# Bias handling in a routed feed-forward: b1 by broadcast DMA and VectorE, b2 by GpSimd, no bias products on TensorE

## The chip, the cores and the metric

The kernel runs on one core of one Trainium2 chip. The metric is the device time in microseconds of one execution. Of several executions the median is given.

## The reference

One transformer block on 2 x 1024 tokens of width 256: cross-attention over 154 context rows (16 heads), then a feed-forward layer with 8 experts, of which each token takes the one with the highest router logit.

```python
x = x + xcond(layernorm(x), ctx, ctx, tau, delta, Wq, bq, Wk, bk, Wv, bv, Wo, bo)
# feed-forward of layernorm(x), DIM = 256, HIDDEN = 1024, E = 8
top1 = jnp.argmax(softmax(x @ router_w + router_b), axis=-1)
for i in range(E):
    h = jnp.einsum('bsd,df->bsf', x, w1[i]) + b1[i]
    a, g = jnp.split(h, 2, axis=-1)
    y = jnp.einsum('bsh,hd->bsd', a * jax.nn.sigmoid(g), w2[i]) + b2[i]
    out = out + jnp.where((top1 == i)[..., None], y, 0.0)
x = x + out
```

## The kernel before

The attention stage takes the first 170 us or so, and a routing stage follows that sorts the tokens by expert. The change hardly touches either. It lies in the feed-forward stage, which begins near 189 us.

Tokens are gathered into 18 tiles of 128 rows (`SLOT_TILES`). Thirteen are **whole**: all rows belong to one expert. Five are **mixed**, at places 2, 5, 8, 11 and 14 (`MIXED_AT`): four pieces of 32 rows, each with an expert of its own. The hidden width of 1024 is cut into four **quarters**; a quarter holds 256 hidden values with their 256 gates. The loop runs n = 0 to 71: all 18 tiles for quarter 0, then for quarter 1 and so on. The weights of one quarter for all experts (8 x 768 KB) are in SBUF, and those of the next are loaded meanwhile by SP (`load_experts`, L662). In quarter 0 SP paces the eight loads for quarter 1 by TensorE's transposes of the gathered tiles (`xin_ready`).

For a whole tile TensorE makes the up product with the hidden values on partitions (L1342). Its bias b1 is then one number for each partition: ScalarE adds it in the sigmoid (L1599), VectorE in the gating (L2022), and the down product (L1380) follows two steps later. ScalarE copies each whole tile's w1 to `w1_now` first (L1565).

For a mixed tile the tokens are on partitions, 32 for each piece, and the weights are the moving operand: the up product is 16 matmuls over four column strips of 32 (L1334), the down product 16 more (L1373). Before each, the pieces' w1 and w2 must be copied out of the quarter's weights to `piece_w1` and `piece_w2`: two pieces by VectorE (L2039, L2042), the others by ScalarE and GpSimd (L881, L884 on GpSimd; in quarter 0 it takes two pieces of the second to fifth mixed tile). VectorE multiplies value by gate to `mixed_u` (L2014), TensorE turns this (L1350), ScalarE copies it to `mixed_ut` (L1607), and the down product runs three steps after the up product. A bias here is a row for each piece, along the free dimension, and there are two ways in which it comes in:

- In quarter 0 both biases come from TensorE. b1 and b2 were split into three bf16 parts by GpSimd (`split_biases`), stored and loaded back to `b_split` by SP. `of_tile`, made by VectorE (L1975), says which of its 24 rows belong to a piece's expert. Four matmuls of 24 rows add the bias ahead of the up product (L1330, 512 columns) and four ahead of the down product (L1369, 256 columns). ScalarE's gate (L1592) and VectorE's `mixed_u` then read the PSUM bank.
- In quarters 1 to 3 SP loads the b1 row of each piece's expert, broadcast to 32 partitions, to `bias_in` (L734). VectorE adds it to the product and writes `hidden` in SBUF (`bias`, L2006). ScalarE's gate (L1587) and `mixed_u` read `hidden`.

The result y adds up in `slot_rows`: VectorE adds each quarter's down product (`add_y`, L2033). For whole tiles b2 comes in during quarter 1: GpSimd adds the expert's row to y (`add_b2`, L907) at step j + 19 for tile j, and VectorE's `add_y` of quarter 1 waits for this.

Each engine runs its own list of instructions in order. GpSimd's list in one step n of the loop is: a gather (L897, until all 18 are done), the copies of w2 and of w1 that are due, `add_b2`, and in the last quarter an output store (L912). An engine's number of an expert is read from SBUF to a register (L877 on GpSimd, L733 on SP) once and then kept.

Of the kernel before, what the change touches and what calls it, by code (L numbers as in the profile page):

```python
# [33 lines left out]
P = 128  # L34
# [48 lines left out]
PARTS = 3  # L83
BIAS_ROWS = PARTS * EXPERTS
TURN_B1, SPLIT_BIASES = (0, 21), (1, 6)
# [31 lines left out]
def constants():  # L117
# [20 lines left out]
        "row_expert": (p % EXPERTS)[:, None] * 1.0,  # L138
# [15 lines left out]
def build(nc, x, ctx_t, tau, delta, wq, bq, wk, bk, wv, bv, wo, bo, rw, rb, weights, b1, b2, const, ones, minus_ones, out,  # L154
# [3 lines left out]
    with ctx:  # L158
# [13 lines left out]
        of_tile = sb("of_tile", [BIAS_ROWS, WHOLE_TILES + MIXED_PIECES], BF16)  # L172
# [81 lines left out]
        biases = sb("biases", [P, P + DIM // HDIM], stack=splitting)  # L254
        biases_rest = sb("biases_rest", [P, P + DIM // HDIM], stack=splitting)
        bias_parts = sb("bias_parts", [P, PARTS, P + DIM // HDIM], BF16, splitting)
# [31 lines left out]
        b_split = sb("b_split", [BIAS_ROWS, 2 * HQ + DIM], BF16)  # L288
# [16 lines left out]
        b1_parts = nc.dram_tensor("b1_parts", (PARTS, P, P), BF16).ap()  # L305
        b2_parts = nc.dram_tensor("b2_parts", (PARTS, P, DIM // HDIM), BF16).ap()
# [17 lines left out]
        s_b2 = sem("s_b2")  # L324
        bias_step = sem("bias_step")
        bias_stored = sem("bias_stored")
        bias_loaded = sem("bias_loaded")
# [161 lines left out]

        def w2_due(n):  # L490

            return [mixed_count(n) - 1] if n >= 0 and mixed(n) else []
# [89 lines left out]
        def _(sp):  # L582

            def store_biases():
                sp.wait_ge(bias_step, 4)
                sp.dma_start(b1_parts.rearrange("w p n -> p w n"), bias_parts[:, :, 0:P]).then_inc(bias_stored, 16)
                sp.dma_start(b1_rows.rearrange("e (m n) -> (e m) n", n=P), biases[:, 0:P]).then_inc(bias_stored, 16)
                sp.dma_start(b2_parts.rearrange("w p n -> p w n"), bias_parts[:, :, P:]).then_inc(bias_stored, 16)

            def load_biases():  # L590
                sp.wait_ge(pv_done, UNITS * CHUNKS)
                sp.wait_ge(bias_stored, 48)
                for w in range(PARTS):
                    at = slice(EXPERTS * w, EXPERTS * (w + 1))
                    sp.dma_start(b_split[at, 0:2 * HQ],
                                 b1_parts[w].rearrange("(q e m) n -> e q (m n)", q=QUARTERS, e=EXPERTS)[:, 0, :]).then_inc(bias_loaded, 16)
                    sp.dma_start(b_split[at, 2 * HQ:],
                                 b2_parts[w].rearrange("(e a) n -> e (a n)", e=EXPERTS)).then_inc(bias_loaded, 16)
# [92 lines left out]
            sp.dma_start(biases[:, P:], b2.rearrange("(p n) -> p n", p=P)).then_inc(s_b2, 16)  # L691
# [44 lines left out]

            sp.dma_start(b2_sb[:, :, :].rearrange("p e n -> p (e n)"),
# [9 lines left out]
        def _(pool):  # L747
# [76 lines left out]
            def split_biases():  # L824
                pool.wait_ge(s_b2, 16)
                pool.wait_ge(b1_copied, 1)
                pool.tensor_copy(bias_parts[:, 0, :], biases[:, :]).then_inc(bias_step, 1)
                pool.wait_ge(bias_step, 1)
                pool.tensor_tensor(biases_rest[:, :], biases[:, :], bias_parts[:, 0, :], ALU.subtract).then_inc(bias_step, 1)
                pool.wait_ge(bias_step, 2)  # L830
                pool.tensor_copy(bias_parts[:, 1, :], biases_rest[:, :]).then_inc(bias_step, 1)
                pool.wait_ge(bias_step, 3)
                pool.tensor_tensor(bias_parts[:, 2, :], biases_rest[:, :], bias_parts[:, 1, :], ALU.subtract).then_inc(bias_step, 1)

# [6 lines left out]
            for c, i in SCHEDULE:  # L841
# [8 lines left out]
                if (c, i) == SPLIT_BIASES:  # L850
                    split_biases()
# [14 lines left out]
            for t in POOL_HOTS:  # L866
                pool.wait_ge(row_known, t // TPC - CHUNKS + 3)
                if t == POOL_HOTS[0]:
                    pool.wait_ge(bias_stored, 48)
# [9 lines left out]

            def copy_w1(k, c):  # L880
                pool.tensor_copy(piece_w1[:, c, :], w1_of_piece(pool, k, expert_of(piece_at(k, c)))).then_inc(w1_pool, 1)  # L881

            def copy_w2(k, c):
                pool.tensor_copy(piece_w2[:, c, :], w2_of_piece(pool, k, expert_of(piece_at(k, c)))).then_inc(w2_pool, 1)  # L884
# [15 lines left out]
            def add_b2(j):  # L900
                at = tile_at(j)
                expert = expert_of(at)
# [3 lines left out]
                y = slot_rows[:, at, DIM:2 * DIM]  # L906
                pool.tensor_tensor(y, y, b2_sb[:, bass.ds(expert, 1), :].rearrange("p o n -> p (o n)"), ALU.add).then_inc(b2_added, 1)  # L907
# [37 lines left out]
        def _(pe):  # L945
# [362 lines left out]
            def expert_rows(at, columns):  # L1308

                return of_tile[:, at:at + 1].to_broadcast([BIAS_ROWS, columns])  # L1310
# [805 lines left out]
```

## Time and profile before

| | |
|---|---|
| median of 3 runs | 412.96 us (412.38 to 413.06) |
| profiled execution, its own time | 413.04 us |
| its span | 411.2 us |
| TensorE busy | 380.7 us (93% of the span) |
| VectorE, ScalarE, GpSimd busy | 258.4, 220.4, 140.2 us |

The engines are called PE (TensorE), PEld (its weight loads), DVE (VectorE), ACT (ScalarE), POOL (GpSimd) and SP. The span is cut into 40 slices of about 10.3 us; a digit is the busy share in tenths, and PEclk the granted TensorE clock in tenths.

```profile
PE   7969999899999888978999999999999999999991
PEclk9979989999999999986999999999999999999996
```

TensorE is full in all slices from the twentieth to the last but one. Its clock falls once, at the turn from routing to feed-forward (slices 18 and 19).

### The profile page before, as it was taken

What the parts mean: (1) busy time and instruction counts of PE and PEld (TensorE: products, weight loads), DVE (VectorE), ACT (ScalarE), POOL (GpSimd) and SP (SyncE); (2) the same over time, 40 slices, a digit from 0 to 9 for tenths busy, and PEclk for the clock granted to TensorE, in tenths of its full rate; (3) what the DMA queues carried; (4) which work ended last, traced back from release to release, by engine and by line L of the source; (5) the groups of instructions that cost most, each with busy time, mean ns of one, the idle gap of its engine ahead of it and who ended that gap; (6) DMA issues with size and microseconds to landing.
All of it is one profiled execution on the core that took longest, in us unless ns stands there. A gap on an engine that the chain in (4) does not pass through costs nothing.

```text
span 411.2 us, 8873 instructions
## 1 busy us (share of the span) xinstructions
PE 380.7 (93%) x2907; PEld 263.1 (64%) x2912; DVE 258.4 (63%) x714; ACT 220.4 (54%) x433; POOL 140.2 (34%) x184
## 2 busy tenths in 40 slices
PE   7969999899999888978999999999999999999991
PEld 3545444456555444766776777887877778877680
DVE  3948985667777863886466634776556553665540
ACT  3314467656655566454555555666556565565540
POOL 5258150031011011367766431433511121155632
PEclk9979989999999999986999999999999999999996
DMA  7563769081101292134856562891039600001111
GB/s 222 127 185 75 146 141 274 6 181 52 50 26 53 84 376 72 63 109 139 313 189 219 152 225 62 301 383 48 27 97 421 175 27 28 0 34 60 38 65 38
DMA packets 29122, 54.33 MB, mean 132 GB/s; under 512 B 8482, under 2 KB 18774, under 8 KB 28950
## 3 DMA queue, kind: packets, MB, share of 16 engines
q1 hardware_dynamic: 25090, 45.72, 35.7%
q0 software_dynamic: 2688, 7.26, 5.5%
q10 hardware_dynamic: 1300, 0.79, 0.9%
q8 instruction: 24, 0.39, 0.4%
q14 instruction: 20, 0.16, 0.1%
HBM read 39.33 MB, written 6.99 MB: 113 GB/s over the span
## 4 chain that ended last, share of the span: by engine, by line
PE 77%; DVE 7%; ACT 4%; issue 4%; SPq 3%; DMA 2%; POOL 1%; another core or an unknown queue 1%; ACTq 0%; DVEq 0%; POOLq 0%
PE bank L1342 22%; PE bank L1380 11%; PE bank L1334 8%; PE bank L1373 5%; PE bank L1064 4%; PE bank L1074 4%; PE bank L1156 4%; PE bank L1013 3%; PE bank L974 3%; PE bank L1052 2%; PE bank L1133 2%; ACT probs L1459 2%; DMA x_sb<-in_x_dram 2%; PE bank L1188 1%; DVE row_max L1729 1%
## 5 line engine op out<-in xcount | busy, mean ns | idle before, releaser
L1342 PEld LDWEIGHTS bank<-slot_rows,w_now 128*128 128x128 f32 x832 | 102.0, 194 | 6.2 <-issue 2.5
L1342 PE MATMUL bank<-slot_rows,w_now 128*128 128x128 f32 x832 | 103.5, 278 | 1.2 <-ACT slot_rows L1550 0.8
L1729 DVE TENSOR_REDUCE row_max<-bank 128x3 f32<-128x462 f32 (+1 forms) x96 | 53.5, 580 | 16.1 <-PE bank L1013 15.7
L2022 DVE SCALAR_TENSOR_TENSOR act_ut<-bank,b_of,gate 128x128 f32<-128x128 f32 x104 | 31.7, 346 | 49.7 <-ACT gate L1599 48.6
L1459 ACT ACTIVATE probs<-bank 128x512 f32<-128x512 f32 x80 | 45.8, 597 | 23.3 <-PE bank L1052 15.5
L1565 ACT ACTIVATE w_now<-w_sb 128x1024 f32 x52 | 54.7, 1054 | 2.7 <-DVE tile_expert L1955 2.1
L1380 PE MATMUL bank<-w_sb,act_ut 128*128 x208 | 54.8, 387 | 0.0
L1599 ACT ACTIVATE gate<-bank,b_of 128x128 f32<-128x128 f32 x104 | 32.3, 364 | 32.8 <-PE bank L1342 29.6
L1380 PEld LDWEIGHTS bank<-w_sb,act_ut 128*128 128x128 f32 x208 | 35.5, 190 | 15.5 <-issue 12.7
L755 POOL TENSOR_SCALAR var<-mv 128x1 f32<-128x1 f32 (+1 forms) x17 | 3.9, 232 | 110.2 <-DVE mv L1766 87.1
L881 POOL COPY piece_w<-w_sb 128x1024 f32 x24 | 25.1, 1057 | 45.1 <-PE bank L1334 43.4
L1334 PE MATMUL bank<-piece_w,slot_rows 128*32 128x512 f32 x320 | 38.8, 597 | 0.0
L1013 PE MATMUL bank<-k_stack,q_stack 99*128 99x154 bf16 x256 | 33.5, 237 | 5.1 <-DMA k_stack<-d_parts 3.9
L1013 PEld LDWEIGHTS bank<-k_stack,q_stack 99*128 99x128 bf16 x256 | 22.4, 102 | 23.8 <-issue 12.8
L884 POOL COPY piece_w<-w_sb 128x512 f32 x24 | 14.4, 610 | 66.3 <-PE bank L1373 66.3
L2033 DVE TENSOR_TENSOR slot_rows<-bank,slot_rows 128x256 f32<-128x256 f32 x72 | 29.9, 415 | 0.6 <-PE bank L1380 0.5
L2039 DVE COPY piece_w<-w_sb 128x1024 f32 x40 | 27.5, 694 | 0.5 <-issue 0.5
L1052 PE MATMUL bank<-q_stack,k_stack 102*128 102x512 bf16 x64 | 24.4, 388 | 0.1
L912 POOL DMA_INDIRECT out_dram<-slot_rows,slot_row x18 | 19.3, 1070 | 11.9 <-DVE slot_rows L2033 8.5
L897 POOL DMA_INDIRECT slot_rows<-rows,slot_row x18 | 20.1, 1119 | 8.0 <-DVE slot_row L1947 3.9
L1587 ACT ACTIVATE gate<-hidden 128x256 f32<-128x256 f32 x15 | 6.3, 417 | 29.5 <-DVE hidden L2006 29.5
L1550 ACT ACTIVATE slot_rows<-bank 128x256 f32<-128x256 f32 x18 | 6.8, 384 | 28.1 <-PE bank L1305 22.1
(205 smaller groups left out, 598.2 us busy)
## 6 DMA issues: line engine op xcount, KB each, us to landing
w_sb<-in_weights_dram SPq DMA_DIRECT2D x32, 768.0 KB, 9.1
q_stack<-q_split SPq DMA_DIRECT2D x18, 256.0 KB, 5.0
rows<-row_buf SPq DMA_DIRECT2D x17, 256.0 KB, 2.6
bias_in<-b_rows SPq DMA_DIRECT2D x60, 64.0 KB, 2.2
x_sb<-in_x_dram SPq DMA_DIRECT2D x4, 512.0 KB, 5.8
b_sb<-in_b_dram SPq DMA_DIRECT2D x1, 1024.0 KB, 8.3
k_stack<-k_split SPq DMA_DIRECT2D x12, 77.0 KB
q_stack<-q_split ACTq DMA_DIRECT2D x6, 128.0 KB, 3.4
```

Source lines behind the costliest of these rows:

```text
L1013: ins = pe.matmul(score_bank(c, i)[:, CTX * n:CTX * (n + 1)], q_stack[0:STACK, stack_slot(c), at, P * t:P * (t + 1)], k_stack[0:STACK, c / ...
L1052: ins = pe.matmul(st_ps[n % 2][:, :], k_stack[0:STACK_T, c // 2, stack_at(4 * g + j), 0:HEAD_ROWS], q_stack[0:STACK_T, stack_slot(c), stac ...
L1334: ins = pe.matmul(h_ps[j % RING][PIECE * c:PIECE * (c + 1), :], slot_rows[:, tile_at(n), P * k + PIECE * c:P * k + PIECE * (c + 1)], piece ...
L1342: ins = pe.matmul(h_ps[j % RING][:, P * m:P * (m + 1)], w1_now[:, whole_count(n) % 2, k, P * m:P * (m + 1)], slot_rows[:, tile_at(n), P * ...
L1380: ins = pe.matmul(y_ps[d % RING][:, 0:DIM], act_ut[:, whole_count(n) % RING, k, :], expert_weights(n, at + DIM * k, at + DIM * (k + 1)), s ...
L1459: act.activation(probs[:, n % PROBS, :], st_ps[n % 2][:, :], ACT.Exp, scale=SCALE).then_inc(probs_ready, 1)
L1565: act.activation(w1_now[:, whole_count(n) % 2, :, :].rearrange("p k n -> p (k n)"), w_sb[:, bass.ds(q % 2 * EXPERTS + experts[tile_at(n)], ...
L1599: ins = act.activation(gate[:, n % 2, m, :], h_ps[j % RING][:, P * (KH + m):P * (KH + m + 1)], ACT.Sigmoid, bias=b1_of[:, q, tile_at(n), K ...
L1729: dve.tensor_reduce(row_max[:, c % 2, m, t, first:first + k], score_bank(c, i)[:, 0:k * CTX].rearrange("p (h s) -> p h s", s=CTX), AX_X, A ...
L2022: ins = dve.scalar_tensor_tensor(act_ut[:, whole_count(n) % RING, m, :], h_ps[j % RING][:, P * m:P * (m + 1)], b1_of[:, q, tile_at(n), m:m ...
L2033: dve.tensor_tensor(y, y_ps[d % RING][:, 0:DIM], y, ALU.add).then_inc(y_added, 1)
L2039: dve.tensor_copy(piece_w1[:, c, :], w1_of_piece(dve, k, experts[at])).then_inc(w1_dve, 1)
```

## The change

Mixed tiles take their biases in quarter 0 without TensorE. b1 comes as in the later quarters: SP loads `bias_in` five more times, interleaved with the first five weight loads of quarter 1, VectorE adds it to `hidden`, and the gate and `mixed_u` of quarter 0 read `hidden`. b2 of mixed tiles is added by GpSimd in quarter 1, in four adds of 32 partitions each, in tile order between those of the whole tiles; each add waits for the one before it, and `add_y` waits for mixed tiles too. The 40 bias matmuls, `of_tile`, the split of the biases into bf16 parts, the two stores and six loads of the parts, and TensorE's wait for them go. `bias_stored` now counts one store instead of three. The diff, cut to its core:

```diff
             def store_biases():
-                sp.wait_ge(bias_step, 4)
-                sp.dma_start(b1_parts.rearrange("w p n -> p w n"), bias_parts[:, :, 0:P]).then_inc(bias_stored, 16)
-                sp.dma_start(b1_rows.rearrange("e (m n) -> (e m) n", n=P), biases[:, 0:P]).then_inc(bias_stored, 16)
-                sp.dma_start(b2_parts.rearrange("w p n -> p w n"), bias_parts[:, :, P:]).then_inc(bias_stored, 16)
...
+                sp.wait_ge(b1_copied, 1)
+                sp.dma_start(b1_rows.rearrange("e (m n) -> (e m) n", n=P), biases[:, :]).then_inc(bias_stored, 16)
...
-            load_biases()
-            for e in range(EXPERTS):
-                sp.wait_ge(xin_ready, 2 * e + 2)
-                load_experts(1, e, e + 1)
...
             def load_bias(k):
                 q, m = divmod(k, MIXED_TILES)
-                if q >= 2:
-                    sp.wait_ge(biased, k - 2 * MIXED_TILES + 1)
+                if q >= 1:
+                    sp.wait_ge(biased, k - MIXED_TILES + 1)
...
+            sp.wait_ge(tables_done, 2)
+            sp.wait_ge(bias_stored, 16)
+            for e in range(EXPERTS):
+                if e < MIXED_TILES:
+                    load_bias(e)
+                sp.wait_ge(xin_ready, 2 * e + 2)
+                load_experts(1, e, e + 1)
...
             def add_b2(j):
...
+                parts = [(expert_of(at), 0, P)] if not mixed(j) else []
+                if mixed(j):
+                    parts = [(expert_of(piece_at(mixed_count(j) - 1, c)), PIECE * c, PIECE * (c + 1)) for c in range(PIECES)]
+                for expert, first, last in parts:
+                    y = slot_rows[first:last, at, DIM:2 * DIM]
+                    if mixed(j):
+                        pool.wait_ge(w1_pool, w1_copies[0])
+                        pool.wait_ge(w2_pool, w2_copies[0])
+                        pool.wait_ge(b2_added, b2_count(j) + first // PIECE)
+                    pool.tensor_tensor(y, y, b2_sb[first:last, bass.ds(expert, 1), :].rearrange("p o n -> p (o n)"), ALU.add).then_inc(b2_added, 1)
+                if mixed(j):
+                    pool.wait_ge(b2_added, b2_count(j + 1))
...
-                if SLOT_TILES + 1 <= n <= 2 * SLOT_TILES and not mixed(n - SLOT_TILES - 1):
+                if SLOT_TILES + 1 <= n <= 2 * SLOT_TILES:
                     add_b2(n - SLOT_TILES - 1)
...
-                    if q == 0:
-                        for c in range(PIECES):
-                            pe.matmul(h_ps[j % RING][PIECE * c:PIECE * (c + 1), :], expert_rows(piece_at(k_mixed, c), PIECE),
-                                      b_split[:, 0:2 * HQ], start=True, stop=False, skip_group_check=True)
...
-                    if first:
-                        for c in range(PIECES):
-                            pe.matmul(y_ps[d % RING][PIECE * c:PIECE * (c + 1), 0:DIM], expert_rows(piece_at(k_mixed, c), PIECE),
-                                      b2_rows, start=True, stop=False, skip_group_check=True)
...
-                if mixed(n) and n >= SLOT_TILES:
-                    act.wait_ge(biased, mixed_count(n) - MIXED_TILES)
+                if mixed(n):
+                    act.wait_ge(biased, mixed_count(n))
...
-                dve.wait_ge(bias_arrived[m], 16 * PIECES * q)
+                dve.wait_ge(bias_arrived[m], 16 * PIECES * (q + 1))
...
-                    dve.tensor_tensor(mixed_u[:, :], h_ps[j % RING][:, 0:HQ] if q == 0 else hidden[:, 0:HQ],
+                    dve.tensor_tensor(mixed_u[:, :], hidden[:, 0:HQ],
...
-                if SLOT_TILES <= n < 2 * SLOT_TILES and not mixed(n):
-                    dve.wait_ge(b2_added, whole_count(n - SLOT_TILES))
+                if SLOT_TILES <= n < 2 * SLOT_TILES:
+                    dve.wait_ge(b2_added, b2_count(n - SLOT_TILES + 1))
...
-                if mixed(n) and n >= SLOT_TILES:
+                if mixed(n):
                     bias(n)
```

## Rows read from the trace of the kernel before

**Rows 1.** Stages: us; busy of PE, PEld, DVE, ACT, POOL; PEclk, DMA share, GB/s.

```profile
189.60:200.03 10.43, 9.74 (x64) 7.29 (x65) 4.66 (x12) 4.21 (x10) 8.25 (x9) 0.84 0.66 227
248.27:298.98 50.71, 50.71 (x432) 39.85 (x432) 32.62 (x75) 30.73 (x60) 17.42 (x22) 1.00 0.47 164
```

**Rows 2.** Instructions of tile b_split: ns min/median/max, first and last start us, form.

```profile
L1330 PE MATMUL bank<-b_split,of_tile x20: 384/384/385, 196.1 to 235.8; 24*32 24x512 bf16 x20
```

**Rows 3.** Timeline of TensorE, first quarter: start us, us, engine, line, instructions.

```profile
205.51 1.09 PE L1373 MATMUL bank<-piece_w,mixed_ut 128*32 128x256 f32 x16
206.85 1.94 PE L1334 MATMUL bank<-piece_w,slot_rows 128*32 128x512 f32 x16
...
242.24 1.95 PE L1342 MATMUL bank<-slot_rows,w_now 128*128 128x128 f32 x16
...
244.33 1.09 PE L1373 MATMUL bank<-piece_w,mixed_ut 128*32 128x256 f32 x16
```

**Rows 4.** Timeline of TensorE, second quarter.

```profile
259.21 1.95 PE L1342 MATMUL bank<-slot_rows,w_now 128*128 128x128 f32 x16
261.09 1.09 PE L1373 MATMUL bank<-piece_w,mixed_ut 128*32 128x256 f32 x16
261.97 1.94 PE L1334 MATMUL bank<-piece_w,slot_rows 128*32 128x512 f32 x16
...
270.23 0.38 PEld L1334 LDWEIGHTS bank<-piece_w,slot_rows 128*32 128x32 f32 x8
```

**Rows 5.** Timeline, start of the feed-forward; in brackets idle before and releaser.

```profile
196.09 0.40 PE L1330 MATMUL bank<-b_split,of_tile 24*32 24x512 bf16 x4
...
198.04 0.38 ACT L1550 ACTIVATE slot_rows<-bank 128x256 f32<-128x256 f32 x1 [3.41 <-remote]
...
200.03 2.02 PE L1342 MATMUL bank<-slot_rows,w_now 128*128 128x128 f32 x16 [0.43 <-ACT w_now L1565]
```

**Rows 6.** Timeline of GpSimd, two of the four operations of the split.

```profile
87.07 0.46 POOL L829 TENSOR_TENSOR biases_rest<-biases,bias_parts 128x144 f32<-128x144 f32 x1
87.60 0.30 POOL L831 CAST bias_parts<-biases_rest 128x144 bf16<-128x144 f32 x1
```

**Rows 7.** Timeline of SP, bias loads of the second quarter; landing of all 60.

```profile
236.55 21.54 SPq L734 DMA_DIRECT2D bias_in<-b_rows  x20
...
DMA to landing us min/median/max: 1.8/2.2/15.0
```

**Rows 8.** VectorE's bias add and its mixed_u, by operands, all four quarters.

```profile
L2006 DVE TENSOR_TENSOR hidden<-bank,bias_in x15: 691/692/693, 255.5 to 390.7; 128x512 f32<-128x512 f32 x15
...
L2014 DVE TENSOR_TENSOR mixed_u<-hidden,gate x15: 424/427/1292, 256.8 to 392.0; 128x256 f32<-128x256 f32 x15
L2014 DVE TENSOR_TENSOR mixed_u<-bank,gate x5: 424/425/426, 200.5 to 239.2; 128x256 f32<-128x256 f32 x5
```

**Rows 9.** Timeline of VectorE and GpSimd, second mixed tile of the first quarter.

```profile
209.09 2.02 POOL L881 COPY piece_w<-w_sb 128x1024 f32 x2 [1.03 <-PE bank L1334]
...
209.90 0.42 DVE L2014 TENSOR_TENSOR mixed_u<-bank,gate 128x256 f32<-128x256 f32 x1 [2.62 <-ACT gate L1592]
...
210.57 0.82 DVE L2042 COPY piece_w<-w_sb 128x512 f32 x1
```

**Rows 10.** Timeline, last mixed tile of the second quarter.

```profile
290.63 1.29 DVE L2014 TENSOR_TENSOR mixed_u<-hidden,gate 128x256 f32<-128x256 f32 x1 [0.54 <-ACT gate L1587]
...
292.00 0.42 PE L1350 MATMUL bank<-consts,mixed_u 128*128 128x128 f32 x2
```

**Rows 11.** GpSimd's adds of b2 to whole tiles.

```profile
L907 POOL TENSOR_TENSOR slot_rows<-slot_rows,b_sb x13: 723/730/918, 243.5 to 291.6; 128x256 f32<-128x256 f32 x13
```

**Rows 12.** Timeline of GpSimd and VectorE, second mixed tile of the second quarter.

```profile
265.20 1.60 POOL L907 TENSOR_TENSOR slot_rows<-slot_rows,b_sb 128x256 f32<-128x256 f32 x2
...
266.47 0.62 DVE L2042 COPY piece_w<-w_sb 128x512 f32 x1
...
267.94 0.68 DVE L2039 COPY piece_w<-w_sb 128x1024 f32 x1
```

More of the change, by code:

```diff
@@ L488, in downs_before, with b2_count @@
             return down_order.index(n)
+        def b2_count(j):
+            return j + (PIECES - 1) * sum(at < j for at in MIXED_AT)
         def w2_due(n):
@@ L1306, in turn_in @@
                 ins.then_inc(xin_ready, 1)
-            def expert_rows(at, columns):
-                return of_tile[:, at:at + 1].to_broadcast([BIAS_ROWS, columns])
             def up(n):
                 q, j = divmod(n, SLOT_TILES)
-                if n >= RING and mixed(n - RING) and n - RING >= SLOT_TILES:
-                    pe.wait_ge(biased, mixed_count(n - RING) - MIXED_TILES)
+                if n >= RING and mixed(n - RING):
+                    pe.wait_ge(biased, mixed_count(n - RING))
                 elif n >= RING:
@@ L1358, in down @@
                 at = KD * 2 * HQ
-                first = n < SLOT_TILES
-                b2_rows = b_split[:, 2 * HQ:]
                 if mixed(n):
@@ L1375, in down @@
                                             piece_w2[:, c, DIM * k:DIM * (k + 1)],
-                                            start=(k == 0 and not first), stop=(k == KH - 1), skip_group_check=True)
+                                            start=(k == 0), stop=(k == KH - 1), skip_group_check=True)
                 else:
@@ L1590, in gates @@
                 act.wait_ge(h_ready, n + 1)
-                if mixed(n):
-                    act.activation(gate[:, n % 2, :, :].rearrange("p m n -> p (m n)"), h_ps[j % RING][:, HQ:2 * HQ],
-                                   ACT.Sigmoid).then_inc(gate_ready, 1)
-                else:
-                    q = n // SLOT_TILES
-                    if j == 0:
-                        act.wait_ge(b1_placed, q + 1)
-                    for m in range(KH):
-                        ins = act.activation(gate[:, n % 2, m, :], h_ps[j % RING][:, P * (KH + m):P * (KH + m + 1)], ACT.Sigmoid,
-                                             bias=b1_of[:, q, tile_at(n), KH + m:KH + m + 1])
-                    ins.then_inc(gate_ready, 1)
+                q = n // SLOT_TILES
+                if j == 0:
+                    act.wait_ge(b1_placed, q + 1)
+                for m in range(KH):
+                    ins = act.activation(gate[:, n % 2, m, :], h_ps[j % RING][:, P * (KH + m):P * (KH + m + 1)], ACT.Sigmoid,
+                                         bias=b1_of[:, q, tile_at(n), KH + m:KH + m + 1])
+                ins.then_inc(gate_ready, 1)
             def copy_ut(n):
@@ L1974, in _ @@
             settle()
-            dve.tensor_scalar(of_tile[:, :], expert_f[0:BIAS_ROWS, :], const_of("row_expert")[0:BIAS_ROWS, :], None, ALU.is_equal)
             dve.tensor_scalar(tile_expert[:, WHOLE_TILES:], expert_f[0:1, WHOLE_TILES:], float(EXPERTS - 1), None,
```

55 lines of the change are left out of this document (10 added, 45 removed).

## The prediction, made before the result was known

> **What bounds the kernel now.** I read the stages first, then one group of three tiles in each stage. The page shows TensorE busy for 93% of the span. By stages it has no idle time from about 200 us on: 50.71 busy of 50.71 in the second quarter, at a granted clock of 1.00, which is the 2.4 GHz level, with VectorE busy 32.62 and GpSimd 17.42 [rows 1]. So in the feed-forward part every nanosecond taken off TensorE is one off the end, as long as no other engine takes its place. The first ten microseconds are the exception (9.74 of 10.43, clock 0.84) [rows 1].
>
> **Part 1: the bias products go.** They run in the first quarter only: 20 with 512 columns (0.384 us each [rows 2]) and 20 with 256. The durations can't be multiplied by 20, because the four of one tile run on four column strips and overlap: four together last 0.40 us [rows 5]. So I take distances between starts, with and without them. The up product of a mixed tile starts 1.34 us after the down product ahead of it in the first quarter (206.85 less 205.51) [rows 3], and 0.88 us in the second, where nothing stands between (261.97 less 261.09) [rows 4]. That is 0.46 for each up product. The down product starts 2.09 us after the whole tile ahead of it (244.33 less 242.24) [rows 3], and 1.88 in the second quarter (261.09 less 259.21) [rows 4]: 0.21 for each.
> - Downs: 5 x 0.21 = 1.05 us. Ups of the second to fifth mixed tile: 4 x 0.46 = 1.84 us. Sum 2.89 us.
> - The first up (n = 2) has no down ahead, so its four are worth at most their 0.40 us, some 0.3. I cost their removal at nothing: the whole tile after it waits for ScalarE's copy of w1, ScalarE stood 3.41 us until 198.04, and TensorE idles 0.43 us there already [rows 5]. It would only idle longer. If that standstill goes, about 0.3 more is gained.
>
> **Part 2: the split, its stores and its loads go.** Four GpSimd operations near 87 us (0.30 and 0.46 us, two of each) [rows 6], two stores and six loads by SP. TensorE's wait for these loads ends nothing I can see: its idle time there ends by other releases. VectorE's `of_tile` goes too, and the pieces' table comes that much earlier, but the first tiles wait for gathers. I take 0 for all of it, between a loss of 0.3 and a gain of 0.3.
>
> **Part 3: b1 of the first quarter by DMA and VectorE.** SP now loads five more broadcast biases, each of four register loads and four DMAs. In the second quarter 20 such pairs took 21.54 us, 1.08 each, with 2.2 us median to landing [rows 7]. From the pieces' table at about 187 us the first four are issued by 191.5 and land by 194. VectorE needs them when the first mixed up product ends, near 198.3 (196.09 + 0.3 + 1.9) [rows 4, 5]. SP is free again before its first weight load of quarter 1, which waits for TensorE's transposes. The other four loads stand between such weight loads, 4.3 us each, and are wanted 10 us later or more. Each also puts 256 KB beside the gathers: the second quarter moves 164 GB/s [rows 1], at which this is 1.6 us of transfer, and the gathers are issued two tiles ahead or more. I take 0; the worst I allow is 1 us at the start.
>
> VectorE adds 0.69 us a mixed tile, ahead of ScalarE's gate [rows 8]. In the first quarter it stands idle 2.62 us ahead of `mixed_u` [rows 9], so the add is covered. What is new is that `mixed_u` then reads `hidden` instead of the bank, and two operands in SBUF meet GpSimd: from the bank it took 0.42 to 0.43 always, from `hidden` up to 1.29 [rows 8], and a copy of w2 took 0.82 where GpSimd copied from 209.09 to 211.11 [rows 9]. In the first quarter `mixed_u` would be issued at about 210.1, some 0.2 later than now, just as GpSimd's second copy starts, and end at 211.4 instead of 210.3. Is that late? In the slowest case of the second quarter it was issued at 290.63, ended at 291.92, and TensorE's turn followed at 292.00 [rows 10]; the turn came 1.37 us after the issue. The same distance here gives 211.5, and TensorE has a whole tile's 16 products to run until 211.7 or so. So 0, with 0.1 to 0.3 a tile if I am off by that much.
>
> **Part 4: b2 of the mixed tiles on GpSimd in the second quarter.** Five tiles, four adds each on 32 partitions. No row shows a 32-partition add. From below I bound it by GpSimd's two-operand step on 144 columns, 0.46 us [rows 6], from above by its longest add of 256 columns, 0.92; I take 0.73, the median of that add, which has the same 256 columns [rows 11]. Each waits for the one before it; such a chain on GpSimd had a gap of 0.07 us (87.07 + 0.46 to 87.60) [rows 6]. Four are thus 3.2 us, with two or three register loads ahead of them. GpSimd was busy 17.42 us of 50.71, about 2.9 of the 8.45 us that three of the 18 tiles take [rows 1]. They fit. Its own copies for the next mixed tile come later, and I cost that at nothing.
>
> The cost lies in the copies that VectorE makes at that time. Now they end at 268.62 (267.94 + 0.68) [rows 12] and the next mixed up product, which needs them, loads its first weights at 270.23 [rows 4]: 1.6 us to spare, 1.8 with the 0.2 that the first copy waits for GpSimd already. A copy issued while GpSimd adds runs on until about 0.29 us after the add ends (266.47 + 0.62 against 265.20 + 1.60) [rows 12], where alone it takes 0.41. So one meeting costs VectorE at most 0.73 - 0.12 = 0.6 us. Four copies meet three or four adds: 1.8 to 2.4 us, so TensorE stalls 0 to 0.6 us. Not every copy is issued just as an add begins, so I take 0.1 us in each of the four groups where copies for a next tile of the quarter follow (the fifth tile's adds meet none that is urgent): 0.4 us.
>
> The Trainium skill, "SBUF — State Buffer", section "Who interferes with whom", says the two engines share a port pair as an exclusive lock, held for a whole instruction, and that VectorE takes part with two SBUF inputs or in its two-port copies. The trace agrees in the copy that ended 0.29 us behind GpSimd's add. The skill's "GPSIMD Engine Reference", section "Architecture", says that each of eight cores serves its own 16 partitions; by this a 32-partition add would be no shorter than a full one. No run here shows that yet.
>
> **The sum.** 413.04 (profiled execution: 411.2 span and 1.84 around it) - 2.89 + 0.4 = 410.55. That execution lies 0.08 above the median of 412.96, so 410.5.
>
> **Rivals.**
> 1. *The port decides (slower).* Four adds delay VectorE's copies one after another at full length, 4 x 0.73 = 2.92 us against 1.6 of room: a stall of 1.3 us in each of four groups, 5.3 us, so 412.96 - 2.89 + 5.3 = 415.4; with adds of 0.92 it would be 8.3, and 418.4. For it: `mixed_u` reached 1.29 [rows 8], three times its time alone. Against: a blocked copy regains 0.12 us, and operations that read a bank take their usual time beside GpSimd (`hidden`, 0.69 [rows 8]). It turns the sign from a stall of 0.72 us a group.
> 2. *The gain is half eaten.* The same stall at 0.3 to 0.5 us, or `mixed_u` turned 0.2 to 0.3 us late five times in the first quarter: 1.2 to 2 us back, 411.3 to 412.1, still faster.
> 3. *No change.* The start loses what the quarter gains: the first bias is late because SP stands as ScalarE did (3.41 us [rows 5]), or a gather is held behind it; ScalarE's gate, and with it the w1 copies, follow. 2 to 3 us, 412.1 to 413.1. For it: SP's register loads at that place are new. Against: some 4 us of room.
>
> That the products stay can't be: the table they read is gone.
>
> **How the numbers follow.** Forecast 410.5 (409.3 to 411.3): 0.56. Rival 2: 0.15. Rival 3, with stalls near 0.7 a group: 0.14. Rival 1: 0.15. A measurement can tell about 0.2%, 0.8 us, from no change. Forecast and rival 2 are faster: 0.71; same 0.14; slower 0.15. The range goes from 409.3 (no stall, and the 0.3 of the first up and the 0.3 of part 2 gained) to 414.0, which leaves out most of rival 1 and little below.
>
> **What would show it.** Part 1: down to up of a mixed tile at 0.88 us in the first quarter, which ends some 2.9 us sooner. Part 3: TensorE without idle time ahead of the second mixed up product, and `mixed_u` done before the turn. Part 4: the second quarter at its 50.71 us, or 0.4 more; a wait of TensorE there for VectorE's piece copies of over 0.7 us a group makes me wrong. Adds on 32 partitions well under or over 0.73 us move the stall, to none or to rival 1.

## The result and the profile of the changed kernel

The changed kernel took 409.01 us (median; 408.98 to 409.12) against 412.67 us for the kernel before beside it. The ratio is 0.9918, interval 0.9897 to 0.9939: 0.8% faster. Forecast were 410.5, between 409.3 and 414.0. The sign held, and the time fell 0.3 us below the range. The profiled execution took 408.98, with a span of 407.2 us; that of the kernel before had 411.2. These 4.0 us are to be explained. Two of the traces taken (after_again, split_back) and some executions fell in a state that makes a whole execution 1.5% or more longer; no figure below is from them.

The feed-forward is cut at the same four events in both traces: the first up product, the start of the second mixed tile's up product, and the first up products of the second and third quarters. Then comes its end. First the kernel before, then the changed one; columns as in [rows 1].

```profile
189.60:206.85 17.25, 16.56 (x130) 12.95 (x130) 8.88 (x23) 8.71 (x21) 12.07 (x12) 0.90 0.75 263
206.85:248.10 41.25, 41.25 (x370) 30.78 (x367) 23.59 (x54) 20.59 (x48) 22.06 (x24) 1.00 0.58 186
248.10:298.82 50.72, 50.72 (x432) 39.85 (x430) 32.63 (x74) 30.74 (x61) 17.42 (x22) 1.00 0.47 164
298.82:401.99 103.17, 103.17 (x869) 80.85 (x867) 59.45 (x152) 60.56 (x118) 31.37 (x34) 1.00 0.27 94
```

```profile
188.58:205.17 16.59, 16.54 (x118) 13.64 (x119) 9.31 (x22) 8.01 (x19) 12.07 (x12) 0.83 0.82 257
205.17:244.15 38.98, 38.98 (x342) 30.53 (x338) 28.17 (x59) 22.26 (x51) 20.48 (x24) 1.00 0.77 253
244.15:294.78 50.63, 50.63 (x431) 39.80 (x430) 35.04 (x74) 30.78 (x61) 33.26 (x40) 1.00 0.44 153
294.78:397.94 103.16, 103.16 (x869) 80.84 (x867) 59.43 (x152) 60.63 (x118) 33.37 (x37) 1.00 0.26 94
```

The second column is the length. Set against the steps of the prediction:

| stretch | before | after | difference | predicted |
|---|---|---|---|---|
| start to first up product | 189.60 | 188.58 | -1.02 | 0 |
| to the second mixed up product | 17.25 | 16.59 | -0.66 | -0.67 (0.46 + 0.21) |
| to the second quarter | 41.25 | 38.98 | -2.27 | -2.22 (3 x 0.46 + 4 x 0.21) |
| second quarter | 50.72 | 50.63 | -0.09 | +0.40 |
| last two quarters | 103.17 | 103.16 | -0.01 | 0 |

Three things are to be seen. The terms of Part 1 came out to 0.05 us in the third row, where TensorE is never idle. The stall of Part 4 isn't there, though GpSimd is busy 33.26 us in the second quarter instead of 17.42. And one microsecond lies ahead of the feed-forward, where the prediction had nothing.

The second row agrees by luck. TensorE's busy time there is almost the same (16.56 and 16.54 us). Up to the first mixed up product the changed kernel lost 0.51 us (7.33 for 6.82): its first two up products took 3.78 and 2.49 us, at a lower clock, against 3.60 and 2.05. It won this back, for the most part, where TensorE no longer stood 0.43 us for ScalarE's copy of w1 [rows 5]. In the changed kernel's third set the stretch is 17.14 us long, with such waits in it again:

```profile
189.36:206.50 17.14, 15.99 (x119) 13.07 (x120) 9.27 (x24) 9.00 (x21) 12.18 (x12) 0.89 0.83 265
```

In the seven traces with both biases moved it is 16.59 to 17.14 us long, in the two of the kernel before 17.25. So the gain there is 0.1 to 0.7 us, according to the waits.

TensorE's timeline of the changed kernel, first quarter, shows what stood in [rows 3]:

```profile
204.29 1.09 PE L1341 MATMUL bank<-piece_w,mixed_ut 128*32 128x256 f32 x16
205.17 1.94 PE L1308 MATMUL bank<-piece_w,slot_rows 128*32 128x512 f32 x16
...
238.50 1.95 PE L1316 MATMUL bank<-slot_rows,w_now 128*128 128x128 f32 x16
240.38 1.09 PE L1341 MATMUL bank<-piece_w,mixed_ut 128*32 128x256 f32 x16
```

From down to up are 0.88 us (1.34 before), from the whole tile to the down product 1.88 (2.09 before). These are the distances of the second quarter in [rows 4], which the prediction took for them.

Of Part 3 the timeline shows SP's first bias load and VectorE's first bias add:

```profile
187.23 3.46 SPq L709 DMA_DIRECT2D bias_in<-b_rows  x4
...
198.50 0.68 DVE L1968 TENSOR_TENSOR hidden<-bank,bias_in 128x512 f32<-128x512 f32 x1
```

And this is what stands in the place of [rows 8], by tile:

```profile
L1968 DVE TENSOR_TENSOR hidden<-bank,bias_in x20: 681/692/693, 198.5 to 386.7; 128x512 f32<-128x512 f32 x20
L1976 DVE TENSOR_TENSOR mixed_u<-hidden,gate x20: 424/426/1257, 199.7 to 387.9; 128x256 f32<-128x256 f32 x20
```

The loads were issued by 190.7 us, and VectorE's add came at 198.50. It had waited for nothing of theirs: it follows `act_ut` of the tile before without a gap. All 20 adds are 0.68 to 0.69 us long. `mixed_u` is slower, as forecast: in the first quarter its five take 0.71, 1.26, 1.26, 1.26 and 0.43 us. The second ends at 209.68, and TensorE turns it at 210.18.

### The profile page after: what moved, and what is told of

It is laid out like the page before. It is cut to its first block, busy times and chain, and to the rows that moved or that the text cites. A ratio compares the mean times of both kernels' runs of the same rounds, so it can differ in the third digit from the quotient of the medians.

```text
span 407.2 us, 8955 instructions
## 1 busy us (share of the span) xinstructions
PE 376.4 (92%) x2872; PEld 262.0 (64%) x2872; DVE 266.6 (65%) x718; ACT 221.5 (54%) x433; POOL 155.5 (38%) x200
## 4 chain that ended last, share of the span: by engine, by line
PE 75%; DVE 11%; DMA 3%; ACT 3%; issue 3%; SPq 3%; POOL 1%; ACTq 0%; DVEq 0%; POOLq 0%
PE bank L1316 24%; PE bank L1348 11%; PE bank L1308 9%; PE bank L1341 5%; PE bank L1056 4%; PE bank L1138 4%; PE bank L1046 3%; DVE row_max L1692 3%; PE bank L995 3%; PE bank L1115 2%; ACT probs L1426 2%; DMA x_sb<-in_x_dram 2%; PE bank L1034 2%; PE bank L956 2%; PE bank L1287 1%
## 5 line engine op out<-in xcount | busy, mean ns | idle before, releaser
L887 POOL TENSOR_TENSOR slot_rows<-slot_rows,b_sb 32x256 f32<-32x256 f32 (+1 forms) x33 | 28.0, 850 | 13.0 <-POOL slot_rows L887 9.0
L2001 DVE COPY piece_w<-w_sb 128x1024 f32 x40 | 28.8, 726 | 0.5 <-issue 0.5
L1554 ACT ACTIVATE gate<-hidden 128x256 f32<-128x256 f32 x20 | 8.3, 417 | 30.3 <-DVE hidden L1968 29.9
L1968 DVE TENSOR_TENSOR hidden<-bank,bias_in 128x512 f32<-128x512 f32 x20 | 13.8, 690 | 15.3 <-PE bank L1308 15.2
```

The costliest lines, as they stand in the source:

```text
L2001: dve.tensor_copy(piece_w1[:, c, :], w1_of_piece(dve, k, experts[at])).then_inc(w1_dve, 1)
```

## The experiments

Ratios are to the kernel before on the same chip, with 95% intervals.

**Both kernels once more.** The kernel before against itself, and the changed kernel in two further sets.

> The kernel before, unchanged, once more and with a trace of its own. Clock theory (the 1.0 us by which the changed kernel reached its first up product sooner, 188.58 against 189.60, comes from where TensorE's clock fell and rose again during attention and routing, and differs from run to run of either kernel): the ratio to the kernel before is 1.000 within 0.002, and the start of the first up product lies at another place than 189.60, anywhere from 188.5 to 190. Rival (removing the split of the biases and its loads brings that 1.0 us): the first up product starts at 189.6 within 0.2 again.

> The changed kernel, unchanged, on one chip with the kernel before. Clock theory: the gain is that of the bias products alone, 2.6 to 3.0 us (ratio 0.9927 to 0.9937). Rival (part 2 brings 1.0 us more): 3.6 to 4.0 us (ratio 0.9903 to 0.9913).

> The changed kernel once more, beside the next three on one chip. Clock theory: from the first up product to the last down product 209.0 us (212.0 in the kernel before); from the start to the first up product 188.6 to 190.5, as in the kernel before (189.6 and 190.5 in its two traces), according to whether TensorE's clock falls a second time between 51 and 62 us. Time 408.7 to 410.8.

The kernel before gave 0.9998 (0.9984 to 1.0012) against itself, the changed kernel 0.9924 (0.9897 to 0.9950) and 0.9902 (0.9886 to 0.9919). So the gain is there in all three sets, 0.8 to 1.0%, or 3.1 to 4.0 us. The expectations missed in part: before_again's first up product, at 190.5 us, lies outside both ranges given, and the two ratios don't decide between the clock and Part 2. The interval of the first holds either's numbers, and 0.9902 is just past the number for Part 2. The next experiment decides.

The traces of these sets say what may be read from one profiled execution. From the second mixed up product on, executions of one kernel agree to 0.02 us: 41.25 and 41.25 before; 38.98 and 39.00 after. Ahead of the feed-forward they don't. One stretch there, 54 to 58 us, in five executions; the column after the five busy times is the granted clock. First the kernel before, at first and again:

```profile
54.00:58.00 4.00, 3.99 (x20) 1.46 (x18) 3.36 (x9) 1.77 (x4) 3.51 (x3) 0.71 0.37 96
54.00:58.00 4.00, 4.00 (x14) 1.82 (x12) 2.77 (x10) 1.52 (x3) 3.03 (x3) 0.50 0.33 85
```

Then the changed kernel, at first and in its third set:

```profile
54.00:58.00 4.00, 3.35 (x26) 1.14 (x26) 4.00 (x7) 2.44 (x5) 3.39 (x3) 1.00 0.63 158
54.00:58.00 4.00, 3.99 (x20) 1.63 (x19) 3.26 (x9) 1.56 (x3) 3.49 (x3) 0.68 0.39 110
```

Last split_back_2, which is described next:

```profile
54.00:58.00 4.00, 3.16 (x26) 0.94 (x23) 4.00 (x7) 2.90 (x5) 3.01 (x2) 1.00 0.75 182
```

The program there is that of the kernel before: nothing that the change adds has run yet. Yet two of these executions are at the 2.4 GHz level throughout (1.00), one is at 1.2 GHz (0.50), and the changed kernel shows 1.00 as well as 0.68. The row of digits shown for the kernel before has it too: 8 tenths in its sixth slice (51 to 62 us) and 7 in its third, so its clock falls more often than once. The first up product starts at 189.60, 190.5, 188.58, 189.4 and 188.1 us in this order: the two at full clock are the two earliest. In all twelve traces the four at 1.00 have it at 188.1 to 189.1 us and the eight at 0.50 to 0.71 at 189.4 to 190.7. The two go together; no run changed the clock alone, so it isn't shown to be the cause. Of the 1.02 us between the first two traces, 0.62 are there by 62 us, as the same instruction of ScalarE shows, before and after, and the rest comes at the routing, between 177 and 189 us:

```profile
61.97 0.60 ACT L1459 ACTIVATE probs<-bank 128x512 f32<-128x512 f32 x1 [0.43 <-PE bank L1052]
61.35 0.60 ACT L1426 ACTIVATE probs<-bank 128x512 f32<-128x512 f32 x1 [0.43 <-PE bank L1034]
```

Matched by this, the kernel before (0.71) and the changed kernel's third set (0.68) have spans of 411.2 and 408.5, 2.7 us apart.

The same by times: the executions of the two kernels that the comparisons used have a mean granted clock of 0.963 to 0.978, and those with 0.974 or more are the shorter ones. Before: 28 of 66, median 412.19 against 413.19. After: 9 of 13, median 408.98 against 410.06. At like clock the change is worth 3.2 and 3.1 us. All four executions of the changed kernel in its first set were of the quick sort, and the 413.04 from which the prediction started was of the other.

**Part 2 put back.** The changed kernel with the split, its three stores, its loads and TensorE's wait for them; `of_tile` stays out.

```
+    split_biases()                              # GpSimd, chunk 1
+    store_biases: three stores; load_biases: the table's loads on SP
+    pe.wait_ge(bias_loaded, 16 * 2 * PARTS)     # ahead of the feed-forward
```

> The changed kernel with the bias split on GpSimd, its two stores, its six loads and TensorE's wait for them put back; nothing reads the parts. Clock theory: the same time as the changed kernel within 0.4 us (ratio to the kernel before 0.992 to 0.995). Rival (part 2 brings 1.0 us): 0.8 to 1.2 us slower than the changed kernel beside it.

> The changed kernel with split, stores, loads and wait put back. Clock theory: 209.0 us from the first up to the last down product, first up product between 188.6 and 190.5, no difference to the changed kernel beyond where the clock falls, 0 to 0.5 us in time. Rival (part 2 is worth about 0.9 us): 0.7 to 1.1 us slower than the changed kernel, and a stretch after 87 us (the split) or after 178 us (the loads) that is longer by that at the same clock.

It gave 0.9935 (0.9912 to 0.9958) beside 0.9924 of the changed kernel, and 0.9903 (0.9886 to 0.9920) beside 0.9902. Its feed-forward has the changed kernel's lengths, 38.98 and 50.62 us. So Part 2 is worth nothing that these runs can tell (their intervals reach 0.7 to 1 us to either side), as predicted. And the earlier start isn't its doing: split_back_2 has the earliest of all, 188.1 us.

**One bias at a time.** b1_alone keeps b2's products on TensorE, b2_alone keeps b1's; both keep the split.

```
b1_alone:  down(): the four products of b2 stay; GpSimd adds b2 to whole tiles only
b2_alone:  up(): the four products of b1 stay; GpSimd adds b2 to all 18 tiles
```

> Only b1 moves: up products of the first quarter without bias products, b2 of mixed tiles still by TensorE with its table, split and loads. The prediction's terms: 4 x 0.46 = 1.84 us less from first up to last down product, 210.2 (209.8 if the first up's 0.3 counts too). Ratio to the kernel before 0.995 to 0.9965.

> Only b2 moves: down products of the first quarter without bias products, the mixed tiles' adds on GpSimd in the second quarter; b1 as before. The prediction's terms: 5 x 0.21 = 1.05 us less, 210.95 from first up to last down product, ratio about 0.9975. If GpSimd's adds cost TensorE the 0.4 us that the prediction took: 211.35.

b1_alone gave 0.9957 (0.9942 to 0.9973), b2_alone 0.9950 (0.9933 to 0.9966). Their traces give clean terms; first the second and third stretch of b1_alone, then of b2_alone:

```profile
206.77:246.78 40.01, 40.01 (x359) 31.20 (x355) 28.08 (x59) 21.82 (x49) 20.46 (x24) 1.00 0.74 244
246.78:297.50 50.72, 50.72 (x432) 39.86 (x431) 32.63 (x74) 30.80 (x61) 17.44 (x22) 1.00 0.42 152
```

```profile
206.81:247.19 40.38, 40.38 (x354) 30.40 (x351) 23.61 (x55) 21.28 (x49) 22.16 (x24) 1.00 0.62 197
247.19:297.82 50.63, 50.63 (x431) 39.79 (x430) 34.99 (x74) 30.75 (x61) 33.26 (x40) 1.00 0.48 165
```

Without b1's products 41.25 becomes 40.01: 1.24 us for three tiles, 0.41 each on average. Without b2's it becomes 40.38: 0.87 for four, 0.22 each. Predicted were 0.46 and 0.21. Together they make 2.11 of the 2.27 us that go when both are gone. The missing 0.16 is one mixed up product in b1_alone's trace, which takes 2.09 us where the others take 1.94:

```profile
216.06 2.09 PE L1342 MATMUL bank<-piece_w,slot_rows 128*32 128x512 f32 x16
```

From one mixed up product to the next it has 9.29, 9.45 and 9.30 us, the kernel before 9.76, so two of the three groups give 0.46, the predicted price. Why the one in the middle took longer isn't shown. Only b2 on GpSimd touches the second quarter, and there it takes 0.09 us off.

By the times b1_alone lies in its expected range, and b2_alone doesn't: 2.1 us were gained where 1.05 was expected. Its feed-forward is 1.23 us shorter in the trace; the rest lies ahead of that, or in the noise.

**How near GpSimd is to the edge.** Three sizes of GpSimd's work for a mixed tile beside the changed kernel's four adds. one_add makes one add on 128 partitions, so the b2 of three pieces is left out. one_more and adds_twice add one, or four, 32-partition adds into a tile that nothing reads, each behind a wait of its own.

```
one_add:     parts = [(expert_of(piece_at(mixed_count(j) - 1, 0)), 0, P)]
one_more:    if first == 0: wait; tensor_tensor(b2_scratch[0:32], y, b2); wait
adds_twice:  the same ahead of each of the four adds
```

> The changed kernel with one 128-partition b2 add for a mixed tile, with the first piece's expert, instead of four of 32 partitions; so the b2 of the other three pieces is left out. GpSimd's group should fall from 8.7 us to about 5.7 (three adds of 0.73 to 1.27 and their gaps of 0.27 fewer). Theory (with four adds GpSimd is late for VectorE, but TensorE never waits): the second quarter, first up to first up, stays at 50.6 us and the ratio to the kernel before stays at 0.990 to 0.992. Rival (the four adds cost TensorE something that no listed wait shows): the quarter shortens by 0.3 us or more and the ratio falls to 0.989 or less.

> The changed kernel with one more 32-partition add for each mixed tile, behind a wait of its own, into a tile that nothing reads. Theory (GpSimd's queue sets the pace as soon as its group is longer than TensorE's 8.47 us): its group becomes 8.7 + 0.75 to 1.2 = 9.5 to 9.9 us; over four groups TensorE loses 4.1 to 5.7 us less the 0.6 to 1.3 that VectorE and the turn have in hand: the second quarter takes 53.4 to 55.7 us instead of 50.63, VectorE's add of mixed y waits longest, and the time is 411.8 to 414.1. Rival (VectorE's piece copies blocked by the port decide): one add in five more blocks at most one copy a tile, under 0.3 us each: the quarter takes at most 51.8.

> The changed kernel with a second add behind a wait for each 32-partition add of b2 (20 more, into a tile that nothing reads). In the changed kernel one group of GpSimd's work in the second quarter takes 8.8 us from one w1 copy to the next (261.09 to 269.89) where TensorE takes 8.47. If GpSimd is next in line there: 1.0 to 1.2 us more for each add, 4 to 5 a group, and after the 5 us that its copies are ahead TensorE stalls in the later groups: 8 to 18 us slower than the changed kernel. If its room is as wide as the prediction had it (2.9 of 8.45 us busy): no more than 1 us slower. The port theory (VectorE's copies blocked by each add) gives VectorE's copies late in the same groups, 2.4 us more a group at most, 5 to 8 us.

| adds for a mixed tile | GpSimd's group, us | second quarter, us | ratio |
|---|---|---|---|
| 1 of 128 partitions | waits for TensorE | 50.62 | 0.9942 (0.9921 to 0.9963) |
| 4 of 32 (the change) | 9.30, 8.80, 8.68 | 50.63 | 0.9902 to 0.9924 |
| 5 of 32 | 9.82, 9.20, 9.19 | 52.27 | 0.9980 (0.9966 to 0.9993) |
| 8 of 32 | 12.33, 11.71, 11.68 | 62.29 | 1.0249 (1.0222 to 1.0276) |

GpSimd's groups go from one copy of w1 to the next, in order; the ratio of the change is from other chips than those of 1 and 5 adds. TensorE's group of three tiles takes 8.47 us. First GpSimd's timeline in the changed kernel, one group of it (in brackets the idle time before and its releaser):

```profile
269.89 1.24 POOL L853 COPY piece_w<-w_sb 128x1024 f32 x1
...
272.27 0.87 POOL L887 TENSOR_TENSOR slot_rows<-slot_rows,b_sb 32x256 f32<-32x256 f32 x1 [0.27 <-POOL slot_rows L887]
273.42 1.19 POOL L887 TENSOR_TENSOR slot_rows<-slot_rows,b_sb 32x256 f32<-32x256 f32 x1 [0.28 <-POOL slot_rows L887]
274.88 0.73 POOL L887 TENSOR_TENSOR slot_rows<-slot_rows,b_sb 32x256 f32<-32x256 f32 x1 [0.28 <-POOL slot_rows L887]
275.88 0.73 POOL L887 TENSOR_TENSOR slot_rows<-slot_rows,b_sb 32x256 f32<-32x256 f32 x1 [0.27 <-POOL slot_rows L887]
277.35 0.73 POOL L887 TENSOR_TENSOR slot_rows<-slot_rows,b_sb 128x256 f32<-128x256 f32 x1 [0.73 <-POOL slot_rows L887]
...
278.57 1.24 POOL L853 COPY piece_w<-w_sb 128x1024 f32 x1
```

The four adds last from 272.27 to 276.61, 4.34 us; the next instruction follows 0.73 us behind. The group from copy to copy is 8.68 us: GpSimd waits for nobody but itself, and loses 0.2 to 0.3 us on TensorE with each group, and 0.8 in the first. The same stretch on VectorE, and TensorE's down product that needs its copies of w2:

```profile
276.72 0.42 DVE L1995 TENSOR_TENSOR slot_rows<-bank,slot_rows 128x256 f32<-128x256 f32 x1 [1.21 <-POOL slot_rows L887]
...
279.16 0.93 DVE L2004 COPY piece_w<-w_sb 128x512 f32 x1
280.01 1.22 DVE L2001 COPY piece_w<-w_sb 128x1024 f32 x1
281.15 0.94 DVE L2004 COPY piece_w<-w_sb 128x512 f32 x1
282.01 0.68 DVE L2001 COPY piece_w<-w_sb 128x1024 f32 x1
...
282.54 1.09 PE L1341 MATMUL bank<-piece_w,mixed_ut 128*32 128x256 f32 x16
```

VectorE's add of y waits for GpSimd's b2 add, 0.66, 0.99, 1.21 and 1.33 us in four successive groups. All that follows in VectorE's order comes later. The last copy of w2 ends at 282.09, and the down product that needs it starts at 282.54: 0.45 us to spare. In the groups before it this was 1.19, 0.85 and 0.65, and in the kernel before, in the second group, 1.53 (268.02 to 269.55). So the delay adds up from group to group, and the quarter ends before the room is used up.

With one add more it is. GpSimd, then VectorE and TensorE in one_more (L892 is the extra add):

```profile
272.09 1.24 POOL L856 COPY piece_w<-w_sb 128x1024 f32 x1
...
274.52 0.80 POOL L892 TENSOR_TENSOR b_scratch<-slot_rows,b_sb 32x256 f32<-32x256 f32 x1 [0.33 <-POOL slot_rows L895]
275.40 0.79 POOL L895 TENSOR_TENSOR slot_rows<-slot_rows,b_sb 32x256 f32<-32x256 f32 x1
276.47 0.86 POOL L895 TENSOR_TENSOR slot_rows<-slot_rows,b_sb 32x256 f32<-32x256 f32 x1 [0.28 <-POOL slot_rows L895]
...
281.28 1.24 POOL L856 COPY piece_w<-w_sb 128x1024 f32 x1
```

```profile
277.00 1.95 PE L1316 MATMUL bank<-piece_w,slot_rows 128*32 128x512 f32 x16
...
279.43 0.42 DVE L2003 TENSOR_TENSOR slot_rows<-bank,slot_rows 128x256 f32<-128x256 f32 x1 [1.32 <-POOL slot_rows L895]
...
283.86 0.94 DVE L2012 COPY piece_w<-w_sb 128x512 f32 x1
...
285.06 1.09 PE L1349 MATMUL bank<-piece_w,mixed_ut 128*32 128x256 f32 x16 [0.24 <-DVE piece_w L2012]
286.19 1.95 PE L1316 MATMUL bank<-piece_w,slot_rows 128*32 128x512 f32 x16
```

TensorE's groups are 9.19 us now (277.00 to 286.19), as GpSimd's are, and it waits for VectorE's copy. The expectation had the order right and the size too large: 9.5 to 9.9 a group was forecast, and the quarter came to 52.27, below its 53.4 and above the rival's 51.8. The extra add lengthened the group by 0.4 to 0.5 us, not by the 0.75 to 1.2 expected: it came with a gap of 0.08 us to the next add of its own piece, and the two adds behind it took 0.79 and 0.86 us instead of 0.87 and 1.19. And only from the third to the fourth and the fourth to the fifth mixed tile were TensorE's groups longer by 0.7 us. adds_twice came out 13 to 14 us slower than the changed kernel, within the 8 to 18 expected of the queue and beyond the 5 to 8 of the port. There the delay reaches TensorE a step earlier:

```profile
274.88 0.42 DVE L2002 TENSOR_TENSOR slot_rows<-bank,slot_rows 128x256 f32<-128x256 f32 x1 [3.84 <-POOL slot_rows L894]
...
277.12 0.44 PE L1331 MATMUL bank<-consts,mixed_u 128*128 128x128 f32 x2 [2.40 <-DVE mixed_u L1983]
```

So the pace is GpSimd's queue; VectorE's wait in program order carries the delay on, and the port adds to it (copies of 0.41 and 0.68 us take 0.93 and 1.22). Rival 1 had the port decide alone; that isn't what was found, though no run takes the port's share away by itself.

At the other end, one_add leaves the second quarter at 50.62: with four adds nothing is lost there. Its ratio was expected at 0.990 to 0.992, and at 0.9942 it is no better than the changed kernel's. The intervals overlap in two of the three sets, and miss by a hair in the third (up to 0.9919). It ran on another chip than these, one on which the changed kernel itself was not run. Its feed-forward is the changed kernel's in the trace (38.98, 50.62), so what differs lies ahead of it; what it is, the runs don't show.

**The clock at the start of the feed-forward.** Idle products in the three waits between the routing and the first up product, in either kernel.

```
-BUSY_BEFORE_PIECES, BUSY_BEFORE_FFN = 4, 2
+BUSY_BEFORE_PIECES, BUSY_BEFORE_FFN = 10, 5
+                if n == 0:
+                    keep_busy(4, o_ps[1])
```

> The changed kernel with more idle matmuls that nothing reads between the routing and the feed-forward: 10 instead of 4 ahead of the piece table, 5 instead of 2 behind it, and 4 new ones between the first transposes and the first up product; they fill waits of 1.36, 0.58 and 0.72 us. Theory (TensorE idles, its granted clock falls to 0.50 and the first two up products take 3.78 and 2.49 us instead of 1.95): they then take about 1.95 each, and 1.5 to 2.3 us are won, less what turns into waits for ScalarE's copies: ratio 0.985 to 0.989. Rival (the start is paced by ScalarE's and VectorE's copies and by the weights): the products are quicker and wait; ratio unchanged at 0.990 to 0.992.

> The kernel before with the same idle matmuls. If the start's clock and the change are independent, the ratio to the kernel before is 0.994 to 0.998 where the changed kernel's gains the same 0.4 to 0.5%, and the two kernels with idle matmuls stand 0.990 to 0.993 to each other: the change's gain without the clock of the start in it. If part of the change's gain was the start, they stand closer.

after_busy gave 0.9949 (0.9933 to 0.9966), before_busy 0.9993 (0.9971 to 1.0015). before_busy doesn't beat the kernel that it was made from, and after_busy has no better ratio than the changed kernel had on other chips. TensorE in after_busy:

```profile
190.74 2.05 PE L1316 MATMUL bank<-slot_rows,w_now 128*128 128x128 f32 x16
...
194.46 0.44 PE L1287 MATMUL bank<-consts,slot_rows 128*128 128x128 f32 x2 [1.45 <-DMA slot_rows<-rows,slot_row]
195.25 2.02 PE L1316 MATMUL bank<-slot_rows,w_now 128*128 128x128 f32 x16 [0.36 <-issue]
```

The first two up products take 2.05 and 2.02 us; in the changed kernel they took 3.78 and 2.49, at a granted clock of 0.50 to 0.67. The time came back as waits, 1.45 us for a gather among them: the start is paced by gathers and copies. So the rival named in the expectation held in its kind, products that are quicker and wait; the ratio of 0.990 to 0.992 that it gave didn't, and gathers it hadn't named.

The two stand only 1.8 us to each other (medians 410.55 and 412.34), not the 2.9 to 4.1 expected. In the profiled executions after_busy gains the same 2.25 and 0.09 us from the second mixed tile on. It loses 0.48 ahead of that, and its first attention scores come at 28.9 us against 27.1 in before_busy. In the other ten executions profiled here they come between 26.3 and 27.7. That execution was also the slowest of after_busy's eleven (411.57), so it doesn't stand for their median, and why the pair lies closer stays open. On this chip one_add too stands closer to the kernel before than the changed kernel did on the others, so the chip may have a part in it.

## Why the prediction was right and where it was wrong

**Part 1 was right by its mechanism.** From the second mixed up product on TensorE has no idle time, and the distances of the second quarter, taken as those without bias products, came back to the hundredth in the first: 2.27 us where 2.22 was summed. The other 0.67 lies in a stretch with waits, and there the sum was met by luck (0.66 in the first pair of traces, 0.1 in another). So the 2.89 us became 2.4 to 2.9. Whether the first up's four products bring nothing can't be read from a stretch that varies by more than they are worth.

**Part 2 was right**: nothing that the intervals can tell, shown by putting it back.

**Part 3 was right.** The loads were early, the adds covered. The price of `hidden` in SBUF is there, as forecast: the first quarter's `mixed_u` was 0.42 to 0.43 us before [rows 8], and three of its five now take 1.26. No turn of TensorE waits for it; the second has 0.5 us to spare.

**Part 4 was wrong in its sum, +0.40 us, where -0.09 was measured.** The length of a 32-partition add was right: 0.73 us where nothing disturbs it. The prediction then had four adds at 3.2 us with gaps of 0.07 [rows 6] and said "they fit". They don't: with gaps of 0.27 and 1.19 for an add that meets VectorE's copies, they take 4.34, and GpSimd's group is longer than TensorE's. The step that failed is the stall: it was priced per meeting, 0.1 us in each of four groups, a figure chosen within bounds and worked out from no row. But such a delay costs nothing until the room is gone. In the group shown three copies were blocked, for 0.5 us each, and VectorE waited 1.2 us for GpSimd, and still 0.45 us was left. The right form of this step is a comparison of two group lengths, 8.7 and 8.47 us, summed over the groups, against the room. The four groups of the change don't use it up. With five adds the quarter lost 1.6 us, and with eight 11.7.

**The start was treated as fixed, and isn't.** The sum began at one execution, 413.04 us, and counted its first 189.6 us as given. That stretch varies by 1 to 2 us between executions of the same kernel, together with the granted clock, and the median of three lay on its longer side. From 412.19, the median of the executions before with the higher mean clock, the prediction's 2.89 us without the stall give 409.30, the lower end of the range; at like clock the change is worth 3.1 to 3.2 us, and where the 0.2 to 0.3 above its terms come from isn't shown. So in the two profiled executions, of the 1.5 us between forecast and result 0.49 is the stall that wasn't there, and 1.02 the start. The range allowed 0.6 us for gains of parts 1 and 2 (its own terms give 409.5 for the lower end, not 409.3) and nothing for the start; that end should have lain 1 us further down. That the changed kernel had the higher mean clock in 9 of 13 executions, the one before in 28 of 66, is not explained: putting Part 2 back left it at 8 of 12, and it may be chance.

**The rivals.** Rival 1 (slower) fell in its mechanism, but its place was right: one more add a tile costs 1.6 us in the second quarter, and four make the kernel 2.5% slower than the one before. Rival 2 asked for `mixed_u` or copies late by 0.2 us or more on TensorE's path; TensorE has no wait for either. Rival 3 asked for a late first bias; VectorE never waited for one. ScalarE's standstill of [rows 5] stayed, with and without the change: its copy of the third tile starts 0.97 to 1.88 us behind the end of the transposes that it copies in eleven executions, and 0.39 in before_busy. In the three with the changed program where this reached 1.47 us (after_third, one_more, after_busy), TensorE idled 0.4 to 0.5 us ahead of the first mixed down product; what holds ScalarE there isn't shown.

## What to carry to other kernels

Where an engine has no idle time, the price of an instruction is read from the distance between the starts of its neighbours, with and without it, in two stages of the same kernel. Work moved to a lighter engine is judged by that engine's group length beside the bound engine's, with the gaps of its waits: as long as it is shorter, or the groups are few, delays on the way cost nothing, and beyond that each group pays the difference. A stretch with waits in it can agree with a sum by luck; only one without idle time tests it. Take the spread of the stages that a change doesn't touch from several executions before setting a range.

## What the runs showed of the hardware

- An add on 32 partitions took as long as one on 128: 0.73 us for 256 columns of either. The Trainium skill, "GPSIMD Engine Reference", section "Architecture", has each core serve its own 16 partitions; the equal times agree with that.
- Chained by a semaphore, GpSimd's adds here stood 0.27 to 0.28 us apart where the next one was of another piece, and 0.07 to 0.08 where it was of the same piece (one_more). 0.73 us passed between the last one of a tile and the next instruction.
- Where they meet, both sides pay: VectorE's copies went from 0.41 to 0.93 us and from 0.68 to 1.22, GpSimd's add from 0.73 to 1.19. The Trainium skill, "SBUF — State Buffer", section "Who interferes with whom", calls the shared port pair an exclusive lock, and the trace agrees: the slowed copies of w2 end 0.28 to 0.29 us behind the GpSimd instruction that they met.
- TensorE's granted clock at 54 to 58 us lay between 0.50 (the 1.2 GHz level) and 1.00 (2.4 GHz) in twelve executions of the same instructions. The feed-forward began at 188.1 to 189.1 us in the four at 1.00, and at 189.4 to 190.7 in the others.
